# A selective scan on one core: more states' B products made turned by ScalarE, fewer by VectorE and GpSimd

## The reference

```
delta = softplus(dt + bias)
h[t] = exp(delta[t] * A[n]) * h[t-1] + (delta[t] * u[t]) * B[n, t]
y[t] = sum over n of h[t] * C[n, t]   (+ D * u[t])
```

## Time and profile before

| | |
|---|---|
| median of 3 runs | 12322.18 us (12321.95 to 12329.25) |
| the profiled execution | 12312.74 us |
| its span, first to last instruction | 12310.8 us |
| mean granted PE clock | 0.956 of 2.4 GHz |
| PE / DVE / ACT / POOL busy | 86% / 88% / 72% / 77% |
| bytes moved by DMA | 2203.72 MB, 179 GB/s on average |

### The profile page before, as it was taken

The page is one execution under the profiler, slowest core; times in us unless marked ns, Lnnn a source line. Parts: engine busy times, 40 slices in busy tenths (PEclk is TensorE's granted clock), DMA queues, the critical chain, the costliest instruction groups (busy, mean ns, idle before and its releaser), DMA issues. The chain is left out here.

```text
span 12310.8 us, 117469 instructions
## 1 busy us (share of the span) xinstructions
PE 10629.6 (86%) x33046; PEld 4749.1 (39%) x33046; DVE 10864.5 (88%) x7695; ACT 8817.2 (72%) x18292; POOL 9515.3 (77%) x4213
## 2 busy tenths in 40 slices
PE   7888888888888888888888888888888888888888
PEld 2443334343344433434334443334433344334443
DVE  7999779997799978999789997899968999689996
ACT  5777667776677766777667776677766777667776
POOL 4999459994599945999459994599936999369993
PEclk9999989999899998999989999999998999999999
DMA  4677446764467644677446774477745677356773
GB/s 140 214 222 214 117 133 215 221 215 110 134 214 222 214 109 139 215 221 214 104 143 215 221 214 101 148 215 219 214 97 149 216 220 215 94 153 215 219 215 91
DMA packets 677497, 2203.72 MB, mean 179 GB/s; under 512 B 165008, under 2 KB 167056, under 8 KB 665424
## 3 DMA queue, kind: packets, MB, share of 16 engines
q1 hardware_dynamic: 676848, 2196.22, 61.3%
HBM read 2098.86 MB, written 67.11 MB: 176 GB/s over the span
## 5 line engine op out<-in xcount | busy, mean ns | idle before, releaser
L1309 POOL TENSOR_TENSOR state<-state,c_sb 128x1024 f32<-128x1024 f32 x3072 | 7180.7, 2363 | 610.5 <-ACT carry L1143 528.5
L1065 PE MATMUL ps<-state,wt 128*128 128x512 f32 x12288 | 5863.5, 614 | 350.5 <-ACT ya L1136 233.4
L1278 DVE TENSOR_TENSOR_SCAN state<-decay,carry,ps 128x1024 f32<-128x1024 f32 x1728 | 4006.7, 2340 | 41.1
L1065 PEld LDWEIGHTS ps<-state,wt 128*128 128x128 f32 x12288 | 2324.5, 196 | 2778.8 <-issue 2105.3
L1199 ACT ACTIVATE decay<-delta,a_neg 128x1024 f32<-128x1024 f32 x2304 | 2638.6, 1146 | 0.2 <-issue 0.2
L1186 ACT ACTIVATE dbu_t<-du_t,b_t 128x128 f32<-128x128 f32 (+1 forms) x8128 | 2301.4, 360 | 0.0
L1143 ACT COPY carry<-state 128x1 f32<-128x1 f32 x3072 | 572.0, 186 | 2136.4 <-DVE state L1278 2127.1
L1265 DVE TENSOR_TENSOR ps<-ps,du 128x1024 f32<-128x1024 f32 x1544 | 1866.2, 1209 | 97.9 <-PE ps L1015 97.6
L1298 POOL TENSOR_TENSOR dbu<-b_sb,du 128x1024 f32<-128x1024 f32 x768 | 1811.5, 2359 | 0.0
L1015 PE MATMUL ps<-parts,sel 114*128 114x512 bf16 (+1 forms) x3088 | 944.7, 388 | 679.6 <-DVE state L1278 673.1
L1278 DVE TENSOR_TENSOR_SCAN state<-ps,carry,dbu 128x1024 f32<-128x1024 f32 x576 | 1343.2, 2332 | 68.1 <-ACT ps L1199 47.6
(11 more groups left out here) (218 smaller groups left out, 9959.1 us busy)
## 6 DMA issues: line engine op xcount, KB each, us to landing
c_sb<-bc SPq DMA_DIRECT2D x2048, 512.0 KB, 4.6
c_sb<-bc SPq DMA_DIRECT2D x2048, 256.0 KB, 5.7
b_sb<-bc SPq DMA_DIRECT2D x512, 512.0 KB, 4.1
b_sb<-bc SPq DMA_DIRECT2D x512, 256.0 KB, 4.0
x_nat<-x SPq DMA_DIRECT2D x17, 1536.0 KB, 14.8
gates<-gate_a SPq DMA_DIRECT2D x8, 2048.0 KB, 6.8
x_tok<-x SPq DMA_DIRECT2D x288, 48.0 KB, 1.9
gn<-gn_t SPq DMA_DIRECT2D x8, 1536.0 KB, 7.1
```

The source lines that it names most:

```text
L1065: mm = pe.matmul(py[:, q * CH:(q + 1) * CH], col("ident"), state[:, slot(g, n), q * CH:(q + 1) * CH], start=(n == 0), stop=False)
L1278: dve.tensor_tensor_scan(state[:, slot(g, n), way], rate, what, 0.0 if fresh else carry[:, n:n + 1], ALU.mult, ALU.add)\
L1309: pool.tensor_tensor(state[:, slot(g, n), :], state[:, slot(g, n), :], c_sb[:, n % CRING, :], ALU.mult).then_inc(S["weighted"], 1)
```

## The change

A table `MADE` gives for each kind of pass and each state who makes its product: `d` DVE, `b` POOL, `t` turned. The first two kinds have 6, 3 and 7 of them (before 8, 4 and 4), the third 7, 4 and 5. In the first chunk of an image states 1 and 3 are DVE's. `TURN_AT` says at which of ACT's steps the two halves of each turned state are made; halves for low states lie in steps 12 to 15 of the chunk before. There are two buffers of turned products (`TRING`), so a first half waits for the turning before last. DU_AT becomes 4, BT_OUT_AT 9, DUT_AT 10, DUT_OUT_AT 11, and SP asks for a row of B 3 states ahead. `SUMS_AT`, `Y_AT` and the rings of states and C rows stay. `b_t` grows to 10 columns a block. For room, `w_xp` leaves its own place: it is stored in DRAM at the start, waited for, and loaded again in `prep_a` of every image, behind the loads of `w_in_sb`; the first `in_proj` waits for it too. The counts that semaphores are compared with come from tables in place of formulas (left out below where nothing else changes).

```diff
-BRING = 1
-B_AHEAD = 4
-POOLED = (3, 7, 11, 15)
-TURNED = slice(1, 16, 4)
-TURNS = tuple(range(1, 16, 4))
+B_AHEAD = 3
+BY_DVE, BY_POOL, TURNED = "dbt"
+MADE = ("dtdtbtdtdtbtdtdb", "dtdtbtdtdtbtdtdb", "dtbdtdbtddtbdtbd")
+TURNS = (slice(1, 15, 2), slice(1, 15, 2), slice(1, 15, 3))
+TURN_AT = ({1: (12, 13), 3: (14, 15), 5: (1, 3), 7: (4, 5), 9: (5, 6), 11: (7, 8), 13: (9, 10)},) * 2 + \
+    ({1: (12, 13), 4: (14, 15), 7: (1, 3), 10: (4, 5), 13: (8, 9)},)
 BLOCKS = 8
-PRE_AT, SOFTPLUS_AT, DU_AT, DELTA_AT = 1, 2, 5, 7
-BT_AT, BT_OUT_AT, DUT_AT, DUT_OUT_AT = 8, 10, 11, 13
+TRING = 2
+PRE_AT, SOFTPLUS_AT, DU_AT, DELTA_AT = 1, 2, 4, 7
+BT_AT, BT_OUT_AT, DUT_AT, DUT_OUT_AT = 8, 9, 10, 11
...
                 sp.wait_ge(S["w_loaded"], 80 + 16 * GROUPS)
+                sp.wait_ge(S["setup_dve"], 7)
+                sp.dma_start(xp_dram, w_xp[:, :, :].rearrange("p i c -> p (i c)")).then_inc(S["w_loaded"], 16)
+                sp.wait_ge(S["w_loaded"], 96 + 16 * GROUPS)
...
+                    sp.dma_start(w_xp[:, :, :].rearrange("p i c -> p (i c)"), xp_dram).then_inc(S["w_in_loaded"], 16)
                     sp.wait_ge(S["gn_ready"], NCH)
...
-                            pe.wait_ge(S["w_in_loaded"], 64)
+                            pe.wait_ge(S["w_in_loaded"], 80)
...
+            def made(g, n):
+
+                return BY_DVE if g == 0 and n in (1, 3) else MADE[g // NSC % 3][n]
...
-                            if n + B_AHEAD in POOLED:
-                                spread_b(T, at, g, POOLED.index(n + B_AHEAD))
-                            if n + B_AHEAD - NS in POOLED and following:
-                                spread_b(following[0], chunk_at(*following), g + 1,
-                                         POOLED.index(n + B_AHEAD - NS))
+                            if n + B_AHEAD < NS:
+                                spread_b(T, at, g, n + B_AHEAD)
+                            elif following:
+                                spread_b(following[0], chunk_at(*following), g + 1, n + B_AHEAD - NS)
...
+                    def spread_b(T, at, g, n):
+
+                        if made(g, n) == BY_POOL:
+                            sp.wait_ge(S["dbu_pooled"], so_far(BY_POOL, g, n) - 1 + CREDIT)
+                            spread_row(T, at, 0, n, b_sb[:, :], "b_in_0")
...
                     def turn_back(g, n):
 
-                        pe.wait_ge(S["dbut_made"], turns(g, n))
+                        pe.wait_ge(S["dbut_made"], so_far(TURNED, g, n))
+                        src = dbu_t[so_far(TURNED, g, n) % TRING]
                         for j in range(BLOCKS):
-                            mm = pe.transpose(pb[n % 2][:, j * 128:(j + 1) * 128], dbu_t[:, j, :], col("ident"))
+                            mm = pe.transpose(pb[n % 2][:, j * 128:(j + 1) * 128], src[:, j, :], col("ident"))
...
-                            if n not in POOLED:
+                            if made(g, n) != BY_POOL:
...
                     def times_b(T, g, n, half):
 
+                        turn = so_far(TURNED, g, n)
                         if half == 0:
...
-                            if turns(g, n) > 1:
-                                act.wait_ge(S["turned"], turns(g, n) - 1)
+                            if turn > TRING:
+                                act.wait_ge(S["turned"], turn - TRING)
...
+                    def turned_products(T, g, at_step, early):
+
+                        for n, halves in TURN_AT[T % 3].items():
+                            for half, when in enumerate(halves):
+                                if when == at_step and (n < when) == early and made(g, n) == TURNED:
+                                    times_b(T, g, n, half)
...
-                                if n == NS - 1:
-                                    times_b(following[0], g + 1, TURNS[0], 0)
-                            if n == 0 and is_turned(g, TURNS[0]):
-                                times_b(T, g, TURNS[0], 1)
-                            for half in range(2):
-                                if n + 2 - half in TURNS[1:]:
-                                    times_b(T, g, n + 2 - half, half)
+                                turned_products(following[0], g + 1, n, True)
+                            turned_products(T, g, n, False)
...
-                            if n + 2 in POOLED:
-                                times_b(T, c, POOLED.index(n + 2))
+                            if n + 2 < NS and made(g, n + 2) == BY_POOL:
+                                times_b(g, n + 2)
```

More of the change, by code:

```diff
@@ L15 @@
 from contextlib import ExitStack
+from itertools import accumulate
 F32 = mybir.dt.float32
@@ L221, in scan_buf @@
         return at(name, [128, SC] if ring is None else [128, ring, SC], F32, first)
-    delta, du, decay, state, c_sb, b_sb, dbu = (scan_buf(n, r) for n, r in (
-        ("delta", 2), ("du", 2), ("decay", 2), ("state", RING), ("c_sb", CRING), ("b_sb", BRING), ("dbu", BRING)))
-    du_t, dbu_t = (at(n, [128, BLOCKS, 128], F32, next(scan_place)) for n in ("du_t", "dbu_t"))
+    delta, du, decay, state, c_sb = (scan_buf(n, r) for n, r in (
+        ("delta", 2), ("du", 2), ("decay", 2), ("state", RING), ("c_sb", CRING)))
+    b_sb, dbu = map(scan_buf, ("b_sb", "dbu"))
+    du_t, dbu_t0, dbu_t1 = (at(n, [128, BLOCKS, 128], F32, next(scan_place)) for n in ("du_t", "dbu_t0", "dbu_t1"))
+    dbu_t = (dbu_t0, dbu_t1)
     yrc = big("yrc", 5 * KB16, DR)
@@ L438, in _ @@
                                                          (DT0 + RANK * g, 2 * g + order, 6 * NS, RANK)):
-                                nc.vector.tensor_copy(w_xp[lo_p:hi_p, i, to:to + count],
-                                                      from_[lo_p:hi_p, st, src, first:first + count])
+                                last = nc.vector.tensor_copy(w_xp[lo_p:hi_p, i, to:to + count],
+                                                             from_[lo_p:hi_p, st, src, first:first + count])
+                last.then_inc(S["setup_dve"], 1)
             @block.tensor
@@ L929, in slot, with so_far, turned_columns @@
                 return (g * NS + n) % RING
[L931 to L941, removed]
+            def made(g, n):
+                return BY_DVE if g == 0 and n in (1, 3) else MADE[g // NSC % 3][n]
+            order_of = [(g, n) for g in range(6 * NSC) for n in range(NS)]
+            counts = {how: list(accumulate((made(g, n) == how for g, n in order_of), initial=0))
+                      for how in (BY_DVE, BY_POOL, TURNED)}
+            def so_far(how, g, n):
+                return counts[how][g * NS + n + 1]
+            def turned_columns(T):
+                return MADE[T % 3].count(TURNED) * len(orders(T))
             def orders(T):
@@ L950, in c_landed, with b_landed @@
                 return (c * (NS // CRING) + (n // CRING + 1)) * (32 if T % 3 == 2 else 16) + before
-            def b_landed(T, c, i):
-                before = sum(32 if t % 3 == 2 else 16 for t in range(T)) * (NSC * NP // BRING)
-                return (c * (NP // BRING) + (i // BRING + 1)) * (32 if T % 3 == 2 else 16) + before
+            def b_landed(g, n):
+                return sum((32 if h // NSC % 3 == 2 else 16) for h, m in order_of[:g * NS + n + 1]
+                           if made(h, m) == BY_POOL)
             with nc.Block() as block:
@@ L1038, in turn_b @@
                             block_cols = parts[own, 2 * (T // 3), span(at * SC + j * 128, 128)]
-                            out_ = pc[:, 8 * j:8 * j + len(TURNS) * count].rearrange("p (i o) -> p i o", o=count)
-                            mm = pe.matmul(out_, block_cols, sel[own, TURNED, first:first + 128 * count:128],
-                                           start=True, stop=True)
+                            states = sel[own, TURNS[T % 3], first:first + 128 * count:128]
+                            out_ = pc[:, 16 * j:16 * j + turned_columns(T)].rearrange("p (i o) -> p i o", o=count)
+                            mm = pe.matmul(out_, block_cols, states, start=True, stop=True)
                         mm.then_inc(S["bt_mm"], 1)
@@ L1198, in steps @@
                             act.wait_ge(S["scanned"], g * NS + n - 1 + CREDIT)
-                            act.activation(pb[n % 2][:, :] if n in POOLED else decay[:, n % 2, :], delta[:, g % 2, :],
+                            act.activation(pb[n % 2][:, :] if made(g, n) == BY_POOL else decay[:, n % 2, :], delta[:, g % 2, :],
                                            ACT.Exp, scale=a_neg[:, T, n:n + 1]).then_inc(S["decayed"], 1)
```

62 lines of the change are left out of this document (31 added, 31 removed).

## The result

The changed kernel takes 12732.0 us (median of 4 runs, 12725.25 to 12737.07), the kernel before 12322.1: ratio 1.0331, 95% interval 1.0313 to 1.0349. It is 3.3% slower. The forecast was 12268 with a range up to 12480, and the slower rival, which had the right place, stopped at 12480. The profiled execution has a span of 12723.4.

A forecast was written before the change was run, and what follows sets the result against it. DVE and Pool were taken as the joint bound. Chunk savings less first-chunk costs gave -59 us for 8 images, plus 5 at the start: -54, so 12258.7 profiled, 12268 as median; range 12010 to 12480.

The forecast's parts named there:

- the slower rival: State 7's turning on PE behind the copy of y, at low clock in three chunks of four: 12480 us, chance 0.28.
- What bounds the kernel: In the scan's chunks DVE and Pool bound together, within a microsecond; ACT has 7 to 12 us to spare.
- the engines' sums: Work per chunk after the change: ACT 42.1 and 44.8 us, against 45 to 47 for DVE.
- The layout by hand: Steps of a chunk laid out across engines: 46.8, 47.7 and 48.6 us for the three kinds.
- clock term: PE's low clock behind the copy of y: up to 1.7 us, charged a third, 0.5 us, in the first two kinds.
- the chain from ACT's carry 7 over Pool to scan 10: Carry 7 about 2 us late; Pool's product for scan 10 ready at 32.9, DVE wanting it at 31.5.
- The second buffer: Second buffer of turned products lets turned states alternate with DVE's; costs no instruction; where PE is late, ACT is too.
- the sum: Chunk changes of -0.45, -0.7 and +0.1 us by kind, with first-chunk and start costs: -54 us in all.
- The du at no cost: DVE's du moved a state earlier costs 0; scan 4 doesn't wait, as the softplus is done at 9.6.
- The c rows: In the third kind c rows queue behind SP's wait for Pool's product: 0 to 1.2 us a chunk, 0.2 taken.
- w_xp: Load through DRAM hidden in every image, at most 2 us; the store at the start 2 to 10 us, 5 taken.
- the first chunk: Two more turnings on PE, partly at low clock, in each image's first chunk: 1 us, range 0 to 3.

The follow-up runs named there:

- experiment 7: Kernel before the change with only ACT's copy of y one step earlier (Y_AT = 5): 12340.8 us, ratio 1.0010.
- experiment 12: Kernel before the change with Pool's product made three states ahead and B rows asked for 5 ahead: 12313.0 us, ratio 0.9997.
- experiment 10: Kernel of experiment 4 with Pool's product made three states ahead instead of two, B rows asked for 4 ahead: 12001.5 us, ratio 0.9742.
- experiment 4: Changed kernel with copy of y and DVE's du each a step earlier, and step 12's second summation behind the turning of state 13: 12195.9 us, ratio 0.9885.
- experiments 9: Kernel of experiment 4 with each half of a turned product cut to fewer activations, three quarters of the scales left out: 11989.1 us, ratio 0.9729.
- experiment 5: Changed kernel with PE repeating the turning of state 5 and spreads of states 5 and 6 while waiting for y: 12576.6 us, ratio 1.0202.
- experiment 2: Changed kernel with DVE's du at step 3 instead of 4: 12619.2 us, ratio 1.0228.
- experiment 1: Changed kernel with ACT's copy of y one step earlier (Y_AT = 5): 12258.7 us, ratio 0.9937.
- experiment 8: Kernel before the change with only w_xp stored in DRAM once and loaded for each image: 12331.9 us, ratio 1.0007.

## Why the prediction was wrong

**What bounds the kernel, and the engines' sums: right.** DVE busy 44.91 in the first kind where the prediction said 44.5; ACT 42.04 for 42.1 and 44.77 for 44.8. In the kernel before, experiment 7 took away PE's waits for y and experiment 12 DVE's waits for Pool's products, and neither gained anything; experiment 10 shows what DVE's relief is worth in the first two kinds when nothing else is late.

**The layout by hand: right to 0.1 us in the first two kinds and 0.4 short in the third, without its clock term.** Its 46.8, 47.7 and 48.6 stand against means of 46.73, 47.62 and 49.00 in experiment 4, and the chain from ACT's carry 7 over Pool to scan 10 is the one that experiments 9 and 10 cut. This is after three edits: the changed kernel by itself has the late du as well, which the layout put at nothing.

**The step that failed: "I charge a third, 0.5 us, in the two kinds in which it counts; the ends are 0 and 1.7".** It was wrong in three ways, all in the paragraph on state 7.
- *How often.* The clock behind the copy of y is low in 160 of 160 chunks. The charge of a third came from three chunks read; the whole trace of before has it in 40 of 56 and 36 of 64 chunks of the two kinds charged, about two thirds. And before's share was no measure for the change: PE's waits for the copies of y grew from 345 to 598 us over the run, and PE's idle time up to the first summation from 3.7, 2.9 and 2.5 to 5.1, 5.1 and 5.5 us (1.4, 1.7 and 2.2 times, where the prediction said more than twice). The time at the low clock in the scans went from 454 to 1251 us. The Trainium skill (TensorE: Matmul & The Clock Gate, What's actually happening) says that the throttled clock is the default and activity releases it. The prediction set that aside as one sentence, though by it the drop would come in every chunk, and the trace agrees.
- *How much.* 1.7 was the price of a slow double summation alone. The turning ran at the low clock too, in 1.91 and 1.75 for 1.04 in the second and third chunk read (1.05 in the first). Experiment 5 puts the low clock at 2.0 us a chunk in the first two kinds. It reaches the chunk over ACT as well: for late turnings ACT waits 1.36 and 0.70 in the first kind, 0.86, 2.57 and 0.32 in the second, and in the third 2.10, with 0.46 for the b values. Added to the layout these give 48.9, 51.5 and 51.2 for 49.21, 50.98 and 51.37. That is a fit to three chunks, within 0.5 us, and no experiment separates ACT's waits from DVE's. The second buffer was costed at nothing because it adds no instruction.
- *Where.* The third kind was left out, as if state 7 had slack there. DVE waited 3.29 us for it in that chunk, after 5.70 us of PE waiting for y, and this kind lost the most. With the copy of y a step earlier it takes 49.04 us in the mean for 51.82.

In the terms of the sum: charged were 0.5, 0.5 and 0.2 on the layout. The means lie 2.8, 3.2 and 3.2 above it. In the first two kinds 2.0 of that is the low clock (experiment 5) and 0.5 and 1.2 the late du (experiment 2); in the third 2.8 go with the earlier copy of y (experiment 1), clock and order together. Each is measured alone, so they need not add up. With the three chunks' own excess over the layout, 2.41, 3.28 and 2.77, in its place the sum gives 12733. This only says that these chunks hold the whole loss: it puts measured lengths in.

**The du at no cost: wrong.** "If the du were late scan 4 would wait, which it doesn't" looked at the softplus. But in DVE's program the wait for Pool's product stands ahead of the du, so the du no longer fills that wait, it follows it (1.31 idle, then 1.2 of work, in the first kind's chunk). Experiment 2: 113 us. Before, the du stood in the step of state 5, a turned one; moving it to the step of a state of Pool's made the difference.

**The c rows, w_xp, the first chunk: small as said.** Over the run Pool waits 1.1 us for c rows, before 68.2, and 1322 us for carries, before 529. For w_xp see experiment 8. The first chunk of an image takes 48.6 us in both traces.

**The slower rival** had the place, the mechanism and its condition (the low clock in three chunks of four, found in all), and 158 us of 410. Its price for the third kind, 1.1 us for late c rows, stood for a cause that the trace doesn't show. That it got 0.28 against 0.32 for the forecast came from the count of low clocks above.

## What to carry to other kernels

Where a change puts a result that somebody awaits into an engine's program, walk the program in front of it: a wait that cost nothing while nobody waited behind it (here the copy of y) becomes the price of every chunk, and moving that wait by one step can be worth more than the whole change. Count how often something happens over the whole trace, not in the three chunks read. Sums by engine say what can be gained; only the laid-out steps, carried through every engine that passes a carry on, say what will be. And a double buffer that costs no instruction still has a price when the reader is late: count the writer's waits on the engine that holds the ring.

## What the runs showed of the hardware

The mean clock doesn't order the kernels: in experiment 1 it is 0.943, lower than before's 0.956, and the kernel is faster. The kernel before has 1078 us at the low clock, 454 of them in the scans. There it has no price: its chunks with a clock of 0.6 or less behind the copy of y take 47.69 and 48.29 us in the first two kinds, and those with 0.9 or more 48.02 and 48.73. In the changed kernel, where DVE and ACT await what PE makes then, the same low clock costs 2.0 us a chunk of those kinds (experiment 5).

Work that computes nothing new brought the clock back in most chunks of experiment 5. In the chunk of the first kind shown 21 matmuls more (x181 for x160; by the program 22) go with 1.00 for 0.97 and 47.66 us for 49.21. But in 18 of 120 chunks of the first two kinds the clock stayed low, and they took 1.4 and 1.5 us more than the changed kernel's.
